# Layer norm of 47 of 49 node chunks inside the edge-group loop of a graph attention layer, and another drain

## The reference

```python
w  = silu(ea @ W1r + b1r) @ W2r + b2r + silu(eb @ W1s + b1s) @ W2s + b2s   # per edge, 128
q  = (x @ Wq)[dst];  k = (x @ Wk)[src];  v = (x @ Wv)[src]                  # 8 heads of 16
alpha = (q * w * k).sum(per head) / 4 * edge_weight
out = segment_sum(alpha * v, dst) / 16
y = (z - mean(z)) / sqrt(var(z) + 1e-5)      with z = x + out               # per node
```

## Time and profile before

| | us |
|---|---|
| median of three executions | 2006.96 (2004.61 to 2007.41) |
| the profiled execution, device time | 2008.97 |
| its span, first to last instruction | 2007.7 |
| busy: TensorE / VectorE / GpSimd / ScalarE | 1712.1 / 1493.2 / 1491.3 / 561.2 |
| mean granted TensorE clock | 0.930 of full |

### The profile page before, as it was taken

How to read it: one execution, slowest core, us unless ns; L and a number is a source line. 1 busy time by engine, 2 the same in 40 slices (tenths; PEclk the granted TensorE clock), 3 DMA queues, 4 the chain that set the end, 5 groups by cost and what they waited for, 6 DMA issues and landing times. The chain is left out here.

```text
span 2007.7 us, 59673 instructions
## 1 busy us (share of the span) xinstructions
PE 1712.1 (85%) x14497; PEld 1256.3 (63%) x14497; DVE 1493.2 (74%) x3815; ACT 561.2 (28%) x956; POOL 1491.3 (74%) x1575
## 2 busy tenths in 40 slices
PE   8798898988988888887888888888887788888886
PEld 7566666666666656665666666666665566666565
DVE  4588787887878777776776767777777777777776
ACT  5322232322222222222222322222222222223223
POOL 6777777777777777777777777777777777777772
PEclk9799999998999989998988989999899998889898
DMA  9855565665566655655555555555556555555544
GB/s 338 267 168 160 165 171 170 170 169 155 169 171 170 170 168 154 170 164 156 167 153 169 161 161 165 156 168 152 169 152 169 169 153 164 155 169 162 159 139 135
DMA packets 194896, 339.98 MB, mean 169 GB/s; under 512 B 81284, under 2 KB 107252, under 8 KB 194548
## 3 DMA queue, kind: packets, MB, share of 16 engines
q0 software_dynamic: 74784, 203.79, 36.5%
q1 hardware_dynamic: 112344, 126.18, 20.8%
q10 hardware_dynamic: 7420, 6.18, 1.0%
HBM read 321.03 MB, written 14.95 MB: 167 GB/s over the span
## 5 line engine op out<-in xcount | busy, mean ns | idle before, releaser
L538 POOL DMA_INDIRECT kvt<-kvtab,srcS x1542 | 1465.9, 951 | 475.1 <-issue 469.3
L621 ACT ACTIVATE hs<-bank,B 128x512 f32<-128x512 f32 x806 | 510.3, 684 | 1399.2 <-PE bank L550 978.7
L723 DVE TENSOR_TENSOR t<-bank,kvt 128x512 f32<-128x512 f32 (+1 forms) x397 | 268.4, 676 | 397.7 <-DMA kvt<-kvtab,srcS 197.6
L573 PE MATMUL bank<-W2r,hs 128*128 128x128 f32 x3224 | 516.3, 308 | 11.7 <-ACT hs L621 11.7
L573 PEld LDWEIGHTS bank<-W2r,hs 128*128 128x128 f32 x3224 | 433.7, 209 | 101.0 <-issue 79.4
L573 PE MATMUL bank<-W2s,hs 128*128 128x128 f32 x3224 | 462.4, 291 | 0.0
L573 PEld LDWEIGHTS bank<-W2s,hs 128*128 128x128 f32 x3224 | 432.0, 208 | 0.0
L588 PE MATMUL bank<-msg,oh 128*32 128x128 f32 x3224 | 180.7, 296 | 235.9 <-DVE accT L669 231.7
L588 PEld LDWEIGHTS bank<-msg,oh 128*32 128x32 f32 x3224 | 72.6, 110 | 426.8 <-issue 426.0
L733 DVE TENSOR_REDUCE bank<-t 128x32 f32<-128x512 f32 x403 | 280.0, 695 | 13.9
L731 DVE TENSOR_TENSOR t<-bank,t 128x512 f32<-128x512 f32 x403 | 273.3, 678 | 18.8 <-PE bank L563 18.4
(11 more groups left out here) (79 smaller groups left out, 487.6 us busy)
## 6 DMA issues: line engine op xcount, KB each, us to landing
eft<-in_ef SPq DMA_DIRECT2D x103, 512.0 KB
kvA<-kvtab ACTq DMA_DIRECT2D x3200, 1.0 KB
kvS<-kvtab SPq DMA_DIRECT2D x2688, 1.0 KB
dbt<-dst SPq DMA_DIRECT2D x102, 384.0 KB
kvt<-kvtab,srcS POOLq DMA_INDIRECT x1542
qwt<-qtab SPq DMA_DIRECT2D x403, 24.0 KB
kvtab<-kvt SPq DMA_DIRECT2D x24, 256.0 KB, 7.0
qtab<-qx SPq DMA_DIRECT2D x12, 384.0 KB, 5.0
```

The lines of the kernel that those rows point to most:

```text
L538: pool.indirect_dma_start(kvt[:, (g - HX) % KS, t, :], None, kvtab, bass.IndirectOffsetOnAxis(ap=srcS[:, g * TG + t:g * TG + t + 1], axis= ...
L573: pe.matmul(WB[g % 2][:, t * D:(t + 1) * D], hs[:, g % HS, j, t * 128:(t + 1) * 128], w2[:, :], start=(j == 0 and t == 0), stop=False, ski ...
L621: act.activation(hs[:, g % HS, j, :], HB[i % 4][:, :], ACT.Silu, bias=B1[:, j:j + 1]).then_inc(m_si, 1)
L723: m = dve.tensor_tensor(t1[:, s, a:b, :], tiles(WB[s][:, :])[:, a:b, :], kv[:, :, 0:D], ALU.mult)
```

## The change

Of the 49 node chunks, 47 are normalised inside the loop at groups fixed beforehand. Chunk c belongs to the group in which its last destination falls if every node had the same number of edges, plus three (`NORM_LAG`), and at least eight after the chunk before (`NORM_GAP`): groups 12, 20, 28 and so on to 391. A table `lim` holds for each group the number of nodes that must be complete by then; the chip compares it with the groups' first destinations, and the flag falls if one is too low.

At its group (called at below), `scat` gets one more matmul, the centring product of the chunk, into columns 128 to 255 of the same PSUM bank, and `collect` copies 256 columns to `partn`. ScalarE squares with a sum at at+5. VectorE makes a first guess of the inverse root from the bits of the variance (at+5) and three Newton steps (at+6 to at+8), 11 operations on one column, each waiting for the one before. ScalarE scales at at+12, SyncE stores 64 KB at at+17. The two last chunks are normalised after the barrier in one batch, with the root as before, stored from two queues.

The drain changes: both last windows, `rel`, `base` and `basep` are made before the product of group NE-2; before that of group NE-1 VectorE does accumulate(NE-4), collect(NE-3) and collect(NE-2); scat uses banks of its own for the last three groups; `basei` is made last. The reloads of `eft` and `dbt` are issued by SyncE inside the loop, as soon as the last first layer and the last query one-hot are done, and awaited before the barrier.

```diff
+NORM_LAG, NORM_GAP = 3, 8
+GUESS, NEWTON = float(0x5F3759DF), 11
+def norm_plan(n_nodes, n_edges, n_groups):
+    at, g = [], 0
+    for c in range(n_nodes // 128):
+        g = max(-(-(c + 1) * 128 * n_edges // (n_nodes * G)) + NORM_LAG, g + NORM_GAP)
+        if g > n_groups - 12:
+            break
+        at.append(g)
+    return at
...
-            dve.tensor_tensor(mm[:, 4:5], mm[:, 2:3], mm[:, 3:4], ALU.add).then_inc(s_bad, 1)
-
+            link(dve.tensor_tensor(mm[:, 4:5], mm[:, 2:3], mm[:, 3:4], ALU.add))
             dve.wait_ge(s_par, n_par)
+            link(dve.tensor_tensor(room[:, :], d0f[0:1, :], limit[:, :], ALU.subtract))
+            link(dve.tensor_reduce(mm[0:1, 7:8], room[:, :], AX.X, ALU.min))
+            link(dve.tensor_scalar(mm[0:1, 8:9], mm[0:1, 7:8], 0.0, None, ALU.is_lt))
+            dve.tensor_tensor(mm[0:1, 4:5], mm[0:1, 4:5], mm[0:1, 8:9], ALU.add).then_inc(s_bad, 1)
...
+            def store(c):
+                sp.wait_ge(m_y, c + 1)
+                sp.dma_start(out[c * 128:(c + 1) * 128, :], partn[:, c % 2, D:2 * D]).then_inc(m_out[c % 2], 16)
...
                 sp_rows(g)
+                if g - 17 in use_n:
+                    store(use_n[g - 17])
+            sp.wait_ge(m_l1, 2 * NE)
+            for q in range(2):
+                features(q, m_ef[q])
+            sp.wait_ge(m_ot, NE)
+            destinations(0, m_db[0])
...
             def strips(g):
-                return HB[NE - 1 - g] if g >= NE - 2 else SB
+                return HB[NE - 1 - g] if g >= NE - 3 else SB
...
+                if g in use_n:
+                    c = use_n[g]
+                    m = pe.matmul(strips(g)[:, D:2 * D], accT[:, c * 128:(c + 1) * 128], centre,
+                                  start=True, stop=True)
                 m.then_inc(m_sc, 1)
...
+            def square(c):
+                g = at_n[c]
+                act.wait_ge(m_part, g + 1)
+                if c >= 1:
+                    act.wait_ge(m_sq, c)
+                act.activation(sq[:, :], partn[:, c % 2, D:2 * D], ACT.Square, scale=D ** -0.5,
+                               accum_out=ss[:, c:c + 1]).then_inc(m_sq, 1)
+            def scale(c):
+                act.wait_ge(m_nw, NEWTON * (c + 1))
+                act.activation(partn[:, c % 2, D:2 * D], partn[:, c % 2, D:2 * D], ACT.Copy,
+                               scale=rs[:, c:c + 1]).then_inc(m_y, 1)
+            for g in range(NE + 12):
+                if g < NE:
+                    silu(g)
+                if g - 5 in use_n:
+                    square(use_n[g - 5])
+                if g - 12 in use_n:
+                    scale(use_n[g - 12])
+                if g < NE:
+                    act_rows(g)
...
+                if g in use_n:
+                    c = use_n[g]
+                    if c >= 2:
+                        dve.wait_ge(m_out[c % 2], 16 * (c // 2))
+                    dve.tensor_copy(partn[:, c % 2, :], strips(g)[:, 0:2 * D]).then_inc(m_part, 1)
...
+            def first_guess(c):
+                v, r = var[:, c:c + 1], rs[:, c:c + 1]
+                dve.wait_ge(m_sq, c + 1)
+                dve.tensor_scalar(v, ss[:, c:c + 1], 1e-5, None, ALU.add).then_inc(m_nw, 1)
+                dve.wait_ge(m_nw, NEWTON * c + 1)
+                dve.tensor_scalar(r.bitcast(i32), v.bitcast(i32), -0.5, GUESS, ALU.mult, ALU.add).then_inc(m_nw, 1)
+            def refine(c, i):
+                v, r = var[:, c:c + 1], rs[:, c:c + 1]
+                n = NEWTON * c + 2 + 3 * i
+                dve.wait_ge(m_nw, n)
+                dve.tensor_scalar(step[:, :], r, r, v, ALU.mult, ALU.mult).then_inc(m_nw, 1)
...
             for g in range(NE):
                 s = g % 2
+                if g == NE - 2:
+                    window(NE - 2)
+                    window(NE - 1)
+                    next_rel()
+                    next_base()
                 if g == NE - 1:
-                    window(g)
-                    next_rel()
+                    accumulate(NE - 4)
+                    collect(NE - 3)
+                    collect(NE - 2)
...
                 if g + 2 < NE:
                     window_T(g + 2)
+                if g - 5 in use_n:
+                    first_guess(use_n[g - 5])
+                for i in range(3):
+                    if g - 6 - i in use_n:
+                        refine(use_n[g - 6 - i], i)
...
             nc.all_engine_barrier(sems_to_clear=sems)
-            destinations(0)
-            for q in range(min(2, NQP)):
-                features(q)
...
+        left = list(range(NN, NC))
...
+            for j, c in enumerate(cs):
+                m = act.activation(rows(b)[:, j, :], bank[b][:, j * D:(j + 1) * D], ACT.Square,
+                                   accum_out=ss[:, c:c + 1])
```

More of the change, by code:

```diff
@@ L39, in groups, with gnn_program @@
     return ng + (-ng) % 4
[L42 removed]
+def gnn_program(nc, n_edges, xT, xN, srcT, dstT, dstB, dst0, cutT, rowS, rowA, ef, w1, b1, w2r, w2s, b2r, b2s, wq, wk, wv, cst, lim, out):
     f32 = mybir.dt.float32
@@ L73, in gnn_program @@
     KT = TG - 1
+    at_n = norm_plan(N, n_edges, NE)
+    use_n = {g: c for c, g in enumerate(at_n)}
+    NN = len(at_n)
     def gathered(g):
@@ L145, in gnn_program @@
         m_part, m_fold = sem("m_part"), sem("m_fold")
+        m_sq, m_nw, m_y = sem("m_sq"), sem("m_nw"), sem("m_y")
+        m_out = [sem(f"m_out{i}") for i in range(2)]
         m_kvS = [sem(f"m_kvS{i}") for i in range(2)]
@@ L185, in gnn_program @@
             s_rows = sem("s_rows")
+            s_ef = [sem(f"s_ef{i}") for i in range(2)]
+            s_db0 = sem("s_db0")
             s_xp, s_xc, s_hp, s_ha, s_hd = [sem(f"s_{n}") for n in ("xp", "xc", "hp", "ha", "hd")]
@@ L209, in gnn_program @@
             n_par = 0
-            for o, i in ((cS[:, :], cst), (W1[:, :], w1),
+            for o, i in ((cS[:, :], cst), (W1[:, :], w1), (limit[:, :], lim),
                          (b2w[:, 0:D], b2r.rearrange("(a n) -> a n", a=1).broadcast_to([3, D])),
@@ L479, in gnn_program @@
         part = sb("part", [128, 2, D], f32)
+        partn = sb("partn", [128, 2, 2 * D], f32)
         hs = sb("hs", [128, HS, 2, G], f32)
@@ new lines, in gnn_program, with rows, columns @@
+        f_t, f_sq, f_sd, f_rs, f_y = [sem(f"f_{n}") for n in ("t", "sq", "sd", "rs", "y")]
+        left = list(range(NN, NC))
+        NL = len(left)
+        batches = [left[i:i + 4] for i in range(0, NL, 4)]
+        assert len(batches) <= 8
+        f_out = sem("f_out")
+        def rows(b):
+            n = len(batches[b])
+            return kvt[:, b, :, :].rearrange("p t f -> p (t f)")[:, 0:n * D].rearrange("p (a f) -> p a f", a=n)
+        def columns(b):
+            return slice(batches[b][0], batches[b][-1] + 1)
@@ new lines, in gnn_program @@
+        for b, cs in enumerate(batches):
+            n = len(cs)
+            dve.wait_ge(f_sd, b + 1)
+            dve.reciprocal(rs[:, columns(b)], var[:, columns(b)]).then_inc(f_rs, 1)
+            dve.wait_ge(f_rs, b + 1)
+            dve.tensor_tensor(rows(b), bank[b][:, 0:n * D].rearrange("p (a f) -> p a f", a=n),
+                              rs[:, columns(b)].rearrange("p (c a) -> p c a", a=1).broadcast_to([128, n, D]),
+                              ALU.mult).then_inc(f_y, 1)
+        no = 0
@@ new lines, in gnn_program @@
+        for b, cs in enumerate(batches):
+            whole = [c for c in cs if c < NF]
+            if whole:
+                sp.wait_ge(f_y, b + 1)
+                sp.dma_start(out[whole[0] * 128:(whole[-1] + 1) * 128, :].rearrange("(c p) f -> p c f", p=128),
+                             rows(b)[:, 0:len(whole), :]).then_inc(f_out, 16)
+                no += 16
+            if len(whole) < len(cs):
+                act.wait_ge(f_y, b + 1)
+                act.dma_start(out[NF * 128:N, :], rows(b)[0:TAIL, len(whole), :]).then_inc(f_out, 16)
+                no += 16
```

221 lines of the change are left out of this document (95 added, 126 removed).

## The result

The changed kernel took **1995.7 us** (median of four, 1994.18 to 1996.43) against 2007.18 (four, 2004.61 to 2007.6) on the same chip: ratio 0.9946, 95% interval 0.9932 to 0.9959, so 8 to 14 us less. Forecast: 1994.5, 1990.3 to 1999.5. The profiled execution took 1996.43 us, its span is 1995.1, 12.6 less than before.

The account below looks back on a forecast made before the run. GpSimd's gathers, one every 1.253 us, bound the group loop; 22.4 us of layer norm after the barrier was exposed. From 2006.96 us, 16.15 saved less 3.3 (drain) and 0.4 (loop, prologue) gave 1994.5, range 1990.3 to 1999.5.

Parts of the forecast that it names:

- Final stage: After the barrier's release (B): two chunks left in one batch, end at B + 6.25 instead of B + 22.4, saving 16.15 us.
- Inside the loop: Group loop: 47 chunks at 3.4 us each fit in the chain's spare time; cost 0, between 0 and 3 us.
- rival 3: In the loop, gathers wait for VectorE's 517 one-column operations; 83 us slower if each is waited out, 2077; chance 0.04.
- Prologue: Before the loop: the `lim` load and four small operations are covered by 3.3 us; cost 0, at most 1 us.
- Drain, transfers: End of loop: early reloads hold up group 401's last gather, used 5.7 us after issue; cost 3.3 us, 0 to 6.
- named signs: Expected in the new profile: gathers every 1.253 us, last near 1974.5, VectorE idle before group 401, barrier at 1988 to 1989.
- Drain, code: End of loop, new order: group 402's product 5.3 us after 401's, tail 5.2; nearly nothing, between 0 and +1.3 us.
- Sum: Whole kernel: 16.15 less 3.3 for the drain and 0.4 for loop and prologue, 12.45 us saved, giving 1994.5.
- Rival 1: Drain: reloads don't hold up gathers, group 401 starts at 1974.1; saving about 15.5 us, 1991.4; chance 0.2.
- Rival 2: Loop or drain: chain delayed more than seen, backlog of 5 to 8 us at 1975; 1999 to 2002; chance 0.12.
- Rival 4: Whole loop: order check fails and it runs 197 times, or squares force table loads of 1.28 us; no-change chance 0.02.

Follow-up runs that it names:

- the four of chip A: Kernel before with reloads moved into the loop, 2011.83 us; changed kernel with reloads behind the barrier, 1994.63, reloads later, 1993.68, no loop norm, 1998.28.
- the first kernel of the table: Changed kernel with reloads issued after the last group's gathered rows landed, on chips B and C: 3123.57 and 3112.88 us, ratios 1.0069 and 1.0107.

## Why the prediction was right

- *Final stage, 16.15 saved:* measured 16.2 in the profiles, the end 6.2 us after the release (6.25 forecast). The steps hold too: scaling at B + 2.8 (2.9), stores at B + 3.2 (3.3). One table load in the setup, one after the barrier, none in the loop. For the copies that fits the Trainium skill's "ScalarE: Activation LUTs", "Table sets: the hidden batching unit", which counts copy among the functions of every set. The page's list there does not name square; that 47 squares between the Silus brought no load either is the trace's word.
- *Inside the loop, 0 (0 to 3):* shown by leaving the norm out, which shortened the gathers' stretch by 1.0 us. What it takes of the chain's spare time was bounded at 3.4 us a chunk; it took 41.5 us (against before) or 50.7 (against the kernel without it) in 1355 us, in which about 34 chunks fall at one per 40 us: 1.2 to 1.5 us each. The bound was two to three times too high, on the safe side; the rest of VectorE's new work ran while it would have waited for TensorE's second layer. That the stretch came out 1.8 us shorter than before was not forecast. In the six traces (the kernels before and after and the four of chip A) it went from 1933.5 to 1936.9 us. The gaps between gathers add up to 470.0 to 470.6 us in each, so nearly all of this is the length of the gathers themselves (see rival 3).
- *Prologue, 0 (at most 1):* the first gather 0.6 us later.
- *Drain, transfers, +3.3 (0 to 6):* the mechanism is shown from both sides, by the reloads alone in the kernel before (4.5 us slower by the medians, 2 to 5.6 by the interval) and by taking them out (VectorE's wait before group 401 gone). The gather's product came after 6.4 us where I took 5.7 from the earlier trace rows, while the last gathers came 1.2 earlier. Product at 1976.56 for 1977.4 forecast. One of the named signs failed by a little: the last gather was to start within 1 us of 1974.5, and did at 1973.34.
- *Drain, code:* this term was too small. From 401's product to 402's are 6.45 us, not 5.3. The prediction reckoned with 3.66 us from the product to the end of the second layer, its row at the full clock. Its other row, 5.04, was of this same group with the clock down, and here it took 5.03. The slower clock is no price of the late gather: the layer took 2.08 and 1.34 us after 6.3 us idle here, 2.08 and 1.35 after 1.69 in the kernel before, 2.08 and 1.42 after 2.45 with the reloads behind the barrier. Only where the reloads alone were moved did the low clock last longer and cost 1.5 us. From 402's product to the last accumulation's end are 4.9 us (5.2). With the product of 401 0.8 us early the misses cancel, and the last accumulation ends at 1987.90, forecast 1987.9: that is luck. Against the old order the new one costs 1.3 us, the upper end of the forecast's 0 to 1.3.
- *Sum:* 12.45 forecast, 12.6 between the two profiled executions, 11.5 between the medians. The large term was right to 0.1 us; the closeness of the whole is in part luck. Loop and prologue gave 1.2 us where 0.4 was charged, and the drain, counted from the last gather, cost 4.8 where 3.3 was: misses of 1.6 and 1.5 us that cancel. By its own terms the upper end of the range is 1999.8 (2006.96 - 16.15 + 6 + 3), not 1999.5; nothing rests on that.
- *Rival 1* (the reloads don't hold up the gathers): refuted, 3.79 us idle before group 401. *Rival 2* (a delayed chain): nothing of it in the loop; in the drain the 1.3 us of the new order are of this kind. *Rival 4:* the loop ran once.
- *Rival 3* (one-column operations hold up gathers): refuted. It decides from 24 ns an operation; leaving all 517 out shortened the gathers' stretch by 1.0 us, 2 ns each. But the prediction is wrong that VectorE alone waits when a gather and a fast form meet. In the kernel before:

```profile
342.08 0.28 DVE L653 TENSOR_TENSOR oh<-cS,rel 128x128 f32<-128x128 f32 x1
```

```profile
342.12 1.06 POOL L538 DMA_INDIRECT kvt<-kvtab,srcS  x1 [0.30 <-issue]
```

A gather takes 0.95 us, and 61 of the 1526 after 60 us take 0.98 to 1.08. Every one of them started 0.03 to 0.19 us after a one-hot operation of VectorE did (L647 or L653). Where L647 started 0.10 to 0.18 us ahead of a gather, or L653 0.04 to 0.12, the gather was always long: 52 of 52, and likewise all in the changed kernel's trace (44 of 44) and in the four of chip A's experiments. No one-column operation is needed for it. In the changed kernel 53 gathers are long in this way, and one more of 1.33 us stands beside the `rel` operation of the drain, which itself takes 1.21 instead of 1.00. In sum the long gathers cost 4.5 us before and 4.3 after. The other way round, 57 of the 60 L647 operations over 400 ns started 0.46 to 0.66 us into a gather. By the Trainium skill's "SBUF — State Buffer", "SBUF: two separate sides", a gather should be locked out while such an operation runs; the traces agree in kind, for both sides, at 0.03 to 0.13 us a gather in the loop, and the medians of the earlier trace rows could not show it.

Open: whether the reload given after the last rows have landed beats 1993.7, since it was run only where the gathers don't set the loop. Also open is the new drain order beyond the one pair of profiles that puts it at 1.3 us. On the other two chips the old order was 10 and 8 us faster than the first kernel of the table, more than the drain holds, and its cause wasn't traced.

## What to carry to other kernels

Work moved under a loop that another engine sets is free for as long as that engine sets it, and costs a part of its own time where it doesn't: read which engine waits for which on each chip before trusting the gain. A transfer that is moved forward to hide it is not free either: look for the last small transfer on the critical path that it will share the queues with, and start the big one behind that. The loss can be longer than the wait itself, where TensorE's clock then stays down (5.2 us for a wait of 3.7 with the reloads alone moved), but it need not be (3.9 us, all of it wait, in the changed kernel). And a drain's sum should take its matmuls from a row at the clock that the drain has.

## What was not expected of the hardware

- The product that needs a 128-row gather started 1.9 us after the gather's issue ended in the quiet drain of the kernel before, and 5.2 to 6.4 us after it beside the 1.4 MB of reloads (four kernels).
- A gather on GpSimd's queue gets 0.03 to 0.13 us longer when a one-hot operation of VectorE started just before it, and the fast form (L647, L743) up to 0.25 us longer when it starts in the middle of a gather.
- The kernel before took 2007 us on chip A, at a granted clock of 0.93, and 3102 and 3082 us on chips B and C, at 0.77. There the queues of ScalarE and SyncE stall now and then: register moves of up to 1.40 us against 29 ns, row loads of up to 1.39 against 0.23, and 0.61 at most. A late supply of instructions would look like this, but that was not tested, nor that it is the cause of the 50% longer time.
- Where GpSimd sets the loop the change gains 0.5% (ratio 0.9946); on chips B and C its variants with three Newton steps lose 0.5 to 1.1%.
